# Two low-rank products of 256 columns for gate and up, their weight chunks paired, and a mixed order of the first sixteen chunks

## The chip, the cores and the metric

The kernel runs on one core of a Trainium2 chip. The metric is the device time of one execution in microseconds (us). Engines are TensorE (PE), VectorE (DVE), ScalarE (ACT), GpSimd (POOL) and SyncE (SP), each with its own instruction stream; SyncE issues most DMAs.

## The reference

Float32 throughout; 1024 tokens of width 512. Weights come as 4-bit NF4 codes (stored as int32) with one scale per 64 inputs, and each carries a low-rank product of rank 16.

```
W   = NF4[codes] * scale per block of 64
lin(x, W, A, B) = x W^T + (x A^T) B^T
q, k, v = lin(x, ...)            # 512 -> 512 each
x1 = x + lin((q + k + v) / 3, W_o, A_o, B_o)
h  = silu(lin(x1, W_gate, ...)) * lin(x1, W_up, ...)     # 512 -> 1792
y  = x1 + lin(h, W_down, ...)                            # 1792 -> 512
...   # then a second quantized layer (512 -> 512), a layer norm, a 4-batch attention
...   # with one head, a layer norm, and a top-16-of-64 mixture of rank-16 experts
```

The change touches only the first part, up to y. What follows it (the tail) is as before.

## The kernel before

The attention weights are folded into one matrix, M1 = (W_q + W_k + W_v)^T W_o^T / 3 + 1, with the low-rank products inside, so that x1 = M1 applied to x. A weight is decoded in **chunks** of 128x512. ScalarE and VectorE build the 16 NF4 levels out of clipped lines: for each chunk VectorE has four operations, `low` (L1469), `mid` (L1475), `clip` (L1482) and `out` (L1491, writes `value`), and ScalarE four that feed them (`bent` and `bank`, L895 and L917). GpSimd then multiplies by the scales (`wf`, L790 or L795; for k it also adds q, L800). There are 62 chunks: o0 to o3; q, k, v for each of four blocks of inputs; then gate, up and down (g, u, d) for fourteen slices f of 128 hidden units, and four chunks f of the second layer. A ring of three holds the codes (`code`, each 256 KB), loaded by SyncE; a slot is free when `mid` and the ScalarE step of `out` of the chunk before in it are done.

A precise product of 512 columns is three matmuls of float32r parts (hi*hi, hi*lo, lo*hi; `product`, L1114). After decoding, a chunk of gate, up or down gets its low-rank term: TensorE writes it to one PSUM bank (`lora`), VectorE adds it (`merge`, L1512 or L1515), ScalarE takes the hi part (`split`, L887) and GpSimd the lo part (L831). A low-rank product waits until the merge of the chunk before has freed the bank. For gate and up it is four matmuls of 128 columns (L1127), with A held as hi and lo rows in `la_gu` and B in `lb_gu`; `bprep` prepares these.

The order on VectorE, ScalarE and GpSimd is one list that all three walk (`vector_order`), on TensorE another (`tensor_order`). In the **front**, TensorE makes for each of the four blocks i: the low-rank sum of q, k, v (L1162), then two matmuls that add (q + k) and v (L1171, L1174) into a bank; `acc` splits it into `wq_hi` and `wq_lo`; twelve matmuls with the o weights and one with the identity give a block of M1; `m1` splits that (`m_hi`, `m_lo`); and nine matmuls (`partial`) apply it to the first 512 tokens. The other half of the tokens follows after the loop. Then come **rounds** f = 0 to 13: TensorE makes gate:2f, up:2f, gate:2f+1, up:2f+1 (12 matmuls each, for the two halves of the tokens), with low-rank products of the next chunks and down products of earlier slices (6 matmuls each) between them. Beside round f the other engines decode g, u and d of slice f+1. A gate or up chunk covers all 512 inputs of one of the two matrices.

## Time and profile before

| | us |
|---|---|
| time, median of 3 runs | 517.43 (516.74 to 517.47) |
| time of the profiled execution | 515.85 |
| its span in the profile | 514.0 |
| TensorE busy in the span | 482.7 |
| VectorE, ScalarE, GpSimd busy | 375.4, 291.0, 276.3 |

The span runs from the first to the last instruction; 1.85 us of the execution lie around it. The profiled execution is 1.58 us shorter than the median of the runs. An instruction's duration includes its pipeline: VectorE's of 128x512 are listed with some 0.68 us, and start 0.60 us apart when nothing is waited for.

### The profile page before, as it was taken

The numbers are of one execution on the slowest core, as the hardware profiler recorded it, in microseconds if no ns is written. First come the engines' busy times: TensorE is split into PE (matmuls) and PEld (weight loads), VectorE is DVE, ScalarE is ACT, GpSimd is POOL, SyncE is SP. The second block draws the span as 40 slices with busy tenths as digits, with TensorE's granted clock in tenths as the row PEclk, the third lists the DMA queues.
The fourth block names the chain that finished last, engine by engine and source line by source line (L and its number), as shares of the span: only waits on it lengthen the run. The fifth ranks groups of instructions, "written<-read, shape, count | busy, mean of one in ns | idle before, by whom it ended". The sixth has DMA issues, their size and how long they took to land.

```text
span 514.0 us, 7457 instructions
## 1 busy us (share of the span) xinstructions
PE 482.7 (94%) x2248; PEld 391.7 (76%) x2248; DVE 375.4 (73%) x707; ACT 291.0 (57%) x539; POOL 276.3 (54%) x255
## 2 busy tenths in 40 slices
PE   2488989999999999999999999999998999999995
PEld 1246668888888888888888888888886788888884
DVE  6979889847897887997979964884567946466433
ACT  6879868756655775765665733636586512333021
POOL 4786766776655775766665754756299210110001
PEclk9999999999999999999999999999999999999998
DMA  7664532613323332332433201730000000000011
GB/s 213 215 238 133 154 85 84 181 46 102 98 74 97 102 114 92 106 119 83 124 104 94 71 1 53 248 141 1 1 1 0 2 1 22 22 20 22 1 42 41
DMA packets 21415, 43.01 MB, mean 84 GB/s; under 512 B 3328, under 2 KB 3456, under 8 KB 21120
## 3 DMA queue, kind: packets, MB, share of 16 engines
q1 hardware_dynamic: 21152, 42.16, 26.6%
q0 software_dynamic: 224, 0.38, 0.3%
q8 instruction: 19, 0.31, 0.2%
q14 instruction: 20, 0.16, 0.1%
HBM read 40.42 MB, written 2.10 MB: 83 GB/s over the span
## 4 chain that ended last, share of the span: by engine, by line
PE 84%; DVE 4%; issue 4%; ACT 3%; POOL 1%; ACTq 0%; DVEq 0%; POOLq 0%
PE bank L1114 74%; PE bank L1282 2%; PE bank L1127 2%; PE bank L1402 1%; PE bank L1174 1%; ACT prob L1070 1%; PE bank L1136 1%; DVE rmax L1666 0%; ACT pT_hi L887 0%; PE bank L1162 0%; DVE bn L1620 0%; DVE pT_lo L1459 0%; PE bank L1315 0%; ACT eb_hi L887 0%; PE bank L1171 0%
## 5 line engine op out<-in xcount | busy, mean ns | idle before, releaser
L790 POOL TENSOR_TENSOR wf<-value,scale 128x512 f32<-128x512 f32 x50 | 64.6, 1291 | 70.4 <-DVE value L1491 70.1
L1114 PE MATMUL bank<-x_hi,gu_hi 128*128 128x512 f32 x224 | 88.5, 395 | 0.0
L1114 PE MATMUL bank<-x_lo,gu_hi 128*128 128x512 f32 x224 | 87.3, 390 | 0.0
L1114 PE MATMUL bank<-x_hi,gu_lo 128*128 128x512 f32 x224 | 87.3, 390 | 0.0
L870 POOL TENSOR_TENSOR rstd<-veps,neg_half 128x1 f32<-128x1 f32 x24 | 13.2, 550 | 110.8 <-issue 104.6
L895 ACT ACTIVATE bank<-code 128x512 f32<-128x512 int32 x124 | 68.7, 585 | 0.0
L1455 DVE TENSOR_TENSOR xs<-bank,xs 128x512 f32<-128x512 f32 x56 | 38.5, 687 | 23.9 <-PE bank L1114 23.4
L1469 DVE SCALAR_TENSOR_TENSOR low<-bent,bank 128x512 f32<-128x512 f32 x62 | 42.3, 682 | 12.0 <-ACT bank L895 7.4
L1114 PEld LDWEIGHTS bank<-x_hi,gu_lo 128*128 128x128 f32 x224 | 42.1, 188 | 8.8
L1114 PEld LDWEIGHTS bank<-x_lo,gu_hi 128*128 128x128 f32 x224 | 42.1, 188 | 7.9
L1114 PEld LDWEIGHTS bank<-x_hi,gu_hi 128*128 128x128 f32 x224 | 42.1, 188 | 7.9
L842 POOL TENSOR_TENSOR h_lo<-act_f,h_hi 128x512 fp32r<-128x512 f32 x28 | 36.3, 1297 | 20.9 <-ACT h_hi L887 20.9
L1482 DVE SCALAR_TENSOR_TENSOR low<-low,bank 128x512 f32<-128x512 f32 x62 | 42.5, 686 | 5.8
L887 ACT ACTIVATE h_hi<-act_f 128x512 fp32r<-128x512 f32 x28 | 17.7, 632 | 47.7 <-DVE act_f L1552 42.4
L1114 PE MATMUL bank<-h_hi,wd_hi 128*128 128x512 f32 x112 | 43.7, 390 | 0.0
L1114 PE MATMUL bank<-h_hi,wd_lo 128*128 128x512 f32 x112 | 43.6, 389 | 0.0
L1114 PE MATMUL bank<-h_lo,wd_hi 128*128 128x512 f32 x112 | 43.6, 389 | 0.0
L1475 DVE SCALAR_TENSOR_TENSOR bank<-code,bank 128x512 f32<-128x512 int32 x62 | 42.6, 687 | 1.1 <-ACT bank L917 0.7
L1491 DVE SCALAR_TENSOR_TENSOR value<-bank,low 128x512 f32<-128x512 f32 x62 | 42.3, 683 | 0.9 <-ACT bank L895 0.8
L895 ACT ACTIVATE bent<-code 128x512 f32<-128x512 int32 x62 | 38.4, 619 | 4.8 <-DMA code<-codes 4.8
L917 ACT ACTIVATE bank<-code 128x512 f32<-128x512 int32 x62 | 36.7, 592 | 3.2 <-DVE low L1482 3.2
L831 POOL TENSOR_TENSOR gu_lo<-wf,gu_hi 128x512 fp32r<-128x512 f32 x28 | 36.8, 1315 | 2.2 <-ACT gu_hi L887 1.9
(228 smaller groups left out, 1163.7 us busy)
## 6 DMA issues: line engine op xcount, KB each, us to landing
code<-codes SPq DMA_DIRECT2D x62, 256.0 KB, 2.7
scale<-scales SPq DMA_DIRECT2D x100, 128.0 KB, 3.0
xs<-xT SPq DMA_DIRECT2D x2, 1024.0 KB, 7.4
ea_raw<-ex_A SPq DMA_DIRECT2D x1, 2048.0 KB, 9.7
eb_raw<-ex_B SPq DMA_DIRECT2D x1, 2048.0 KB, 8.7
out<-rows SPq DMA_DIRECT2D x8, 256.0 KB, 2.0
bgu_raw<-loB_gu SPq DMA_DIRECT2D x1, 896.0 KB, 5.8
wqkv_raw<-w_qkv SPq DMA_DIRECT2D x1, 768.0 KB, 4.3
```

The costliest lines, as they stand in the source:

```text
L790: pool.tensor_tensor(w, v, scale[:, i % RING_CODES, :], ALU.mult).then_inc(scaled_done, 1)
L831: pool.tensor_tensor(lo, shaped(c, merged_at(c)), hi.bitcast(F32), ALU.subtract).then_inc(lo_done, 1)
L842: pool.tensor_tensor(h_lo[:, f % RING_H, hs], act_f[:, n % 2, :], h_hi[:, f % RING_H, hs].bitcast(F32), ALU.subtract).then_inc(hlo_done, 1)
L887: nc.scalar.activation(dst, src, ACT.Copy).then_inc(done, 1)
L895: nc.scalar.activation(dst, src, ACT.Prelu, bias=float(start), scale=float(slope), alpha=float(alpha)).then_inc(done, 1)
L917: nc.scalar.activation(mid_ps[:, :], code[:, j % RING_CODES, :], ACT.Relu, bias=float(RELU_MID[1]), scale=float(RELU_MID[0])).then_inc(mid ...
L1114: last = nc.tensor.matmul(ps, a, b, start=start and i == 0 and n == 0, stop=stop and i == len(terms) - 1 and n == 2)
L1455: nc.vector.tensor_tensor(xs[:, b, o, :], down_bank(gi, n)[:, :], xs[:, b, o, :], ALU.add)\
L1469: nc.vector.scalar_tensor_tensor(low[:, j % 2, :], bent[:, j % 2, :], float(BEND_LOW[3] - BEND_LAST[3]), last_ps[:, :], ALU.add, ALU.min). ...
L1475: nc.vector.scalar_tensor_tensor(mid_ps[:, :], code[:, j % RING_CODES, :], float(CODE_SHIFT), mid_ps[:, :], ALU.add, ALU.max).then_inc(mid ...
L1482: nc.vector.scalar_tensor_tensor(lj, lj, float(BEND_LAST[3]), mid_ps[:, :], ALU.add, ALU.min)\
L1491: nc.vector.scalar_tensor_tensor(value[:, j % 2, :], top_ps[:, :], float(BEND_TOP[3]), low[:, j % 2, :], ALU.add, ALU.max).then_inc(value_ ...
```

## The change

Five things.

1. **Pairing.** A gate or up chunk of slice f no longer holds one matrix for all inputs: chunk g holds both matrices for inputs 0 to 255, chunk u both for inputs 256 to 511. Each gate and up product waits for chunk g, makes six matmuls, waits for chunk u, and makes six more.
2. **Low-rank products.** With a chunk that holds both matrices, one stationary part of A serves 256 columns of B (gate and up side by side): two matmuls of 256 columns instead of four of 128. B is prepared in parts of three slices (`bprep` 1 to 5, of 128x768 or less) instead of two (128x512 and 128x1280), loaded as needed; A is half as wide.
3. **Order of the later chunks.** g2 moves ahead of round 1 and each g of slice f+2 stands beside round f, so the order beside round f is u, d of slice f+1 and g of slice f+2. Round 12 then has six half chunks beside it where it had eight. The order of round 1 changes too: `bprep` 2 goes ahead of g2, and merges and splits of g2 and u2 move up.
4. **Front order.** The first sixteen chunks are o0 o1 q0 o2 k0 o3 v0 and then q, k, v of blocks 1 to 3, with omerge, osplit, acc and m1 at other places; TensorE makes all nine matmuls of `partial` behind the two accumulating ones instead of three before them.
5. **Front loads.** The codes of the first sixteen chunks use four slots; the scales of o0 to o3 are issued one chunk at a time; x comes in eight pieces of 256 KB instead of two of 1 MB; A and B of o are loaded first and have a semaphore of their own; loads for gate, up and down come later and in smaller pieces.

```diff
+LAST_BEATS = [2, 0, 2, 0, 1, 0, 1, 0]
+def beside_round(f):
+    chunks = [("u", f + 1), ("d", f + 1), ("g", f + 2)]
+    return [c for c in chunks if c[1] < NF]
 def chunk_list():
-    chunks = [("o", k) for k in range(KT)] + [(m, i) for i in range(KT) for m in "qkv"]
-    chunks += [("g", 0), ("u", 0), ("g", 1), ("u", 1), ("d", 0), ("d", 1)]
+    chunks = [("o", 0), ("o", 1), ("q", 0), ("o", 2), ("k", 0), ("o", 3), ("v", 0)]
+    chunks += [(m, i) for i in range(1, KT) for m in "qkv"]
+    chunks += [("g", 0), ("u", 0), ("g", 1), ("u", 1), ("d", 0), ("d", 1), ("g", 2)]
     for f in range(1, NF):
-        chunks += [(m, f + 1) for m in "gud"] if f + 1 < NF else []
+        chunks += beside_round(f)
...
+FRONT = 4 * KT
+RING_FRONT = 4
...
-LB_FIRST = 4
-XSPLIT_AFTER = [6, 7, 8, 9, 11, 12, 13, 14]
+LB_PART = 3
+XSPLIT_AFTER = [7, 9, 10, 12, 13, 15]
+EXTRA_LOADS = {6: ["x0"], 8: ["x1"], 9: ["x2"], 11: ["x3"], 12: ["x4"], 13: ["x5", "gate_a"], 14: ["gate_b0"],
+               15: ["x6"], 16: ["x7"], 18: ["down"]}
+PART_LOADS = {("d", 0): 1, ("g", 3): 2, ("u", 6): 3, ("u", 9): 4}
...
     order.append(("low", CHUNKS[0]))
-    for j in range(4 * KT):
-        half(CHUNKS[j], 0)
+    merge_at = {2: 0, 3: 1, 5: 2, 7: 3}
+    for j in range(FRONT):
+        order.append(("mid", CHUNKS[j]))
+        if j in merge_at:
+            order.append(("omerge", merge_at[j]))
+        if j in (10, 13):
+            order.append(("m1", (j - 10) // 3))
+        order += [("clip", CHUNKS[j]), ("low", CHUNKS[j + 1])]
+        if j in merge_at:
+            order.append(("osplit", merge_at[j]))
+        if j in (8, 11, 14):
+            order.append(("acc", (j - 8) // 3))
+        order.append(("out", CHUNKS[j]))
         if j == 3:
             order.append(("eyes", 0))
-        half(CHUNKS[j], 1)
         if j in XSPLIT_AFTER:
             order.append(("xsplit", XSPLIT_AFTER.index(j)))
-    due.clear()
     def alone(c, *parts):
         for part in parts or (0, 1):
             half(c, part)
         due.clear()
-    alone(("g", 0))
-    order.append(("acc", KT - 1))
-    alone(("u", 0), 0)
-    order.append(("bprep", 0))
-    alone(("u", 0), 1)
-    order += [("bprep", 1), ("m1", KT - 1)]
-    alone(("g", 1), 0)
-    order += [("x1", 0), ("x1", 1)]
+    order += [("mid", ("g", 0)), ("m1", KT - 2), ("clip", ("g", 0)), ("low", ("u", 0)), ("out", ("g", 0)), ("xsplit", 6),
+              ("mid", ("u", 0)), ("acc", KT - 1), ("clip", ("u", 0)), ("low", ("g", 1)), ("out", ("u", 0)), ("bprep", 0),
+              ("mid", ("g", 1)), ("clip", ("g", 1)), ("m1", KT - 1), ("bprep", 1), ("xsplit", 7), ("x1", 0), ("x1", 1)]
...
-    order.append(("silu", 0))
+    order += [("silu", 0), ("bprep", 2)]
...
-    alone(("d", 2), 0)
-    order += [("hsplit", 1), ("low", ("g", 3)), ("split", ("d", 1)), ("out", ("d", 2)), ("silu", 2)]
-    due += [[2, ("merge", ("d", 2))], [3, ("split", ("d", 2))]]
-    order += [("merge", ("g", 2)), ("split", ("g", 2)), ("h", 2), ("merge", ("u", 2)), ("hsplit", 2), ("silu", 3),
-              ("split", ("u", 2)), ("bprep", 2)]
+    order += [("mid", ("d", 2)), ("merge", ("g", 2)), ("clip", ("d", 2)), ("hsplit", 1), ("low", ("g", 3)),
+              ("split", ("d", 1)), ("out", ("d", 2)), ("split", ("g", 2)), ("silu", 2), ("mid", ("g", 3)),
+              ("merge", ("u", 2)), ("clip", ("g", 3)), ("h", 2), ("split", ("u", 2)), ("hsplit", 2), ("silu", 3)]
+    due += [[1, ("merge", ("d", 2))], [2, ("split", ("d", 2))]]
+    half(("g", 3), 1)
...
+        if f in (3, 6, 9):
+            order.append(("bprep", 2 + f // 3))
...
-        for step, count in zip(steps, BEATS[len(halves)]):
+        for step, count in zip(steps, LAST_BEATS if f == NF - 2 else BEATS[len(halves)]):
...
-            beside = [*ahead[:2], None, None]
+            beside = [("g", 2), ahead[0], ahead[1], None]
         elif late:
-            beside = [ahead[0], ahead[1], ahead[2], None]
+            beside = [*ahead, None] if len(ahead) == 3 else [ahead[0], None, ahead[1], None]
...
+        code_fourth = at("code_fourth", 128, [P, 512], I32)
...
+            for j in range(RING_FRONT):
+                load_code(j)
+                if j >= 2:
+                    load_scale(CHUNKS[j - 2])
+            for j, c in enumerate(CHUNKS):
+                if j < RING_FRONT:
+                    continue
+                for name in EXTRA_LOADS.get(j, []):
+                    load_extra(name)
+                if c in PART_LOADS:
+                    load_extra(f"gate_b{PART_LOADS[c]}")
...
+                sp.wait_ge(mid_done, code_before(j) + 1)
+                sp.wait_ge(top_ready, code_before(j) + 1)
+                load_code(j)
+                if j == 5:
+                    load_scale(("o", 2))
+                elif j == 6:
+                    load_scale(("o", 3))
+                elif j >= FRONT:
+                    load_scale(c)
...
+            pool.dma_start(la_o[:, :], loA_o).then_inc(olora_in, 16)
+            pool.dma_start(lb_o[:, :], loB_o).then_inc(olora_in, 16)
             pool.dma_start(sc_qkv[:, :, :], scales_qkv).then_inc(sqkv_in, 16)
             pool.dma_start(ident[:, :], eye).then_inc(eye_in, 16)
-            pool.dma_start(la_o[:, :], loA_o).then_inc(lora_in, 16)
-            pool.dma_start(lb_o[:, :], loB_o).then_inc(lora_in, 16)
...
-                    pe.wait_ge(bprep_done, 2 if k < LB_FIRST else 3)
-                    for h in range(KT):
-                        last = nc.tensor.matmul(lora_ps[:, h * P:(h + 1) * P],
-                                                la_gu[:, "gu".index(kind), h * P:(h + 1) * P],
-                                                lb_gu[:, k * P:(k + 1) * P], start=True, stop=True)
+                    pe.wait_ge(bprep_done, 2 + k // LB_PART)
+                    for h in range(2):
+                        m = 2 * "gu".index(kind) + h
+                        last = nc.tensor.matmul(lora_ps[:, 2 * h * P:2 * (h + 1) * P], la_gu[:, m * P:(m + 1) * P],
+                                                lb_gu[:, k // LB_PART % 2, k % LB_PART, :, :], start=True, stop=True)
...
-                if i:
-                    pe.wait_ge(m1hi_done, i)
-                    pe.wait_ge(m1lo_done, i)
-                    pe.wait_ge(xhi_done, i)
-                    pe.wait_ge(xlo_done, i)
-                    partial(i - 1, 0)
...
                 if i:
-                    partial(i - 1, 1)
-                    partial(i - 1, 2)
+                    pe.wait_ge(m1hi_done, i)
+                    pe.wait_ge(m1lo_done, i)
+                    pe.wait_ge(xhi_done, i)
+                    pe.wait_ge(xlo_done, i)
+                    for r in range(KT - 1):
+                        partial(i - 1, r)
...
-                pe.wait_ge(hi_done, split_no(("gu"[g], f)))
-                pe.wait_ge(lo_done, split_no(("gu"[g], f)))
                 s, ps = f % RING_GU, unit_ps[m % 3][:, :]
-                product(ps, [(gu_hi[:, s, g, k, :], gu_lo[:, s, g, k, :], x1_hi[:, k, tk], x1_lo[:, k, tk])
-                             for k in range(KT)]).then_inc((gate_ready, unit_ready)[g], 1)
+                for h in range(2):
+                    pe.wait_ge(hi_done, split_no(("gu"[h], f)))
+                    pe.wait_ge(lo_done, split_no(("gu"[h], f)))
+                    last = product(ps, [(gu_hi[:, s, k, g, :], gu_lo[:, s, k, g, :], x1_hi[:, k, tk], x1_lo[:, k, tk])
+                                        for k in (2 * h, 2 * h + 1)], start=h == 0, stop=h == 1)
+                last.then_inc((gate_ready, unit_ready)[g], 1)
...
+            half = slice(2 * "gu".index(kind), 2 * "gu".index(kind) + 2)
+            codes.append(cg[:, cut].reshape(2, P, KT, P).transpose(3, 2, 0, 1)[:, half].reshape(P, H))
```

On SyncE at the start of the program the issues stand so before:

```order
L707 DMA code<-codes 128x512 x3
L736 DMA scale<-scales 64x512 x6
L728 DMA code<-codes 128x512
L736 DMA scale<-scales 64x512 x2
L728 DMA code<-codes 128x512 x3
L711 DMA xs<-xT 128x4x512
L728 DMA code<-codes 128x512 x2
```

and so after the change:

```order
L748 DMA code<-codes 128x512 x3
L757 DMA scale<-scales 64x512 x2
L748 DMA code_fourth<-codes 128x512
L757 DMA scale<-scales 64x512 x2
L748 DMA code<-codes 128x512 x2
L757 DMA scale<-scales 64x512 x2
L765 DMA xs<-xT 128x512
L748 DMA code<-codes 128x512
L757 DMA scale<-scales 64x512 x2
L748 DMA code_fourth<-codes 128x512
```

The fourth codes go out behind one pair of scales instead of three, and pieces of x stand between the codes.

On VectorE, in the last block of the front, from `mid` of chunk v3 on, before (L1530 is m1:2, L1459 is acc:3):

```order
L1475 SCALAR_TENSOR_TENSOR bank<-code,bank 128x512
L1482 SCALAR_TENSOR_TENSOR low<-low,bank 128x512
L1469 SCALAR_TENSOR_TENSOR low<-bent,bank 128x512
L1491 SCALAR_TENSOR_TENSOR value<-bank,low 128x512
L1530 SCALAR_TENSOR_TENSOR m_lo<-bank,m_hi 128x512
L1475 SCALAR_TENSOR_TENSOR bank<-code,bank 128x512
L1482 SCALAR_TENSOR_TENSOR low<-low,bank 128x512
L1469 SCALAR_TENSOR_TENSOR low<-bent,bank 128x512
L1491 SCALAR_TENSOR_TENSOR value<-bank,low 128x512
L1459 TENSOR_TENSOR wq_lo<-bank,wq_hi 128x512
```

and after the change, from the same `mid`:

```order
L1544 SCALAR_TENSOR_TENSOR bank<-code_fourth,bank 128x512
L1551 SCALAR_TENSOR_TENSOR low<-low,bank 128x512
L1538 SCALAR_TENSOR_TENSOR low<-bent,bank 128x512
L1560 SCALAR_TENSOR_TENSOR value<-bank,low 128x512
L1544 SCALAR_TENSOR_TENSOR bank<-code,bank 128x512
L1599 SCALAR_TENSOR_TENSOR m_lo<-bank,m_hi 128x512
L1551 SCALAR_TENSOR_TENSOR low<-low,bank 128x512
L1538 SCALAR_TENSOR_TENSOR low<-bent,bank 128x512
L1560 SCALAR_TENSOR_TENSOR value<-bank,low 128x512
L1544 SCALAR_TENSOR_TENSOR bank<-code,bank 128x512
L1528 TENSOR_TENSOR wq_lo<-bank,wq_hi 128x512
```

Both splits have moved one operation later, so that they wait less for TensorE.

On ScalarE, the stretch from the SiLU of gate:8 (the first act_f) to that of gate:9, beside round 4, before:

```order
L994 ACTIVATE act_f<-bank 128x512
L895 ACTIVATE bent<-code 128x512
L895 ACTIVATE bank<-code 128x512 x2
L917 ACTIVATE bank<-code 128x512
L887 ACTIVATE h_hi<-act_f 128x512
L887 ACTIVATE wd_hi<-wf 128x512
L895 ACTIVATE bent<-code 128x512
L895 ACTIVATE bank<-code 128x512 x2
L917 ACTIVATE bank<-code 128x512
L887 ACTIVATE gu_hi<-wf 128x512
L994 ACTIVATE act_f<-bank 128x512
```

and after the change:

```order
L1062 ACTIVATE act_f<-bank 128x512
L960 ACTIVATE bent<-code 128x512
L960 ACTIVATE bank<-code 128x512 x2
L982 ACTIVATE bank<-code 128x512
L952 ACTIVATE h_hi<-act_f 128x512
L952 ACTIVATE gu_hi<-wf 128x512
L960 ACTIVATE bent<-code 128x512
L960 ACTIVATE bank<-code 128x512 x2
L982 ACTIVATE bank<-code 128x512
L952 ACTIVATE gu_hi<-wf 128x512
L1062 ACTIVATE act_f<-bank 128x512
```

Before, this stretch splits d4 and then g5; after the change it splits g5 and then u5, so the split of u5 stands where that of g5 stood.

## Rows read from the trace of the kernel before

**Rows 1.** Busy time by stretch; each engine's us and (xinstructions).

```profile
core 0: us, PE busy (x) PEld busy (x) DVE busy (x) ACT busy (x) POOL busy (x), PEclk, DMA share, GB/s
0.00:66.50 66.50, 43.65 (x139) 27.00 (x139) 53.84 (x90) 54.32 (x103) 46.17 (x47) 1.00 0.61 189
66.50:367.00 300.50, 300.02 (x1405) 249.98 (x1406) 238.57 (x386) 182.58 (x333) 192.16 (x157) 1.00 0.31 94
367.00:514.00 147.00, 138.99 (x706) 114.72 (x704) 83.02 (x233) 54.10 (x104) 37.98 (x52) 0.99 0.04 15
```

**Rows 2.** Waits of TensorE: engine line waited for: us, times, longest.

```profile
PE bank L1155 <- DMA lb_qkv<-loB_qkv: 9.4, 1, 9.4
PE bank L1171 <- POOL wf L800: 7.6, 1, 7.6
...
PE bank L1114 <- DVE wq_lo L1459: 1.7, 2, 1.5
```

**Rows 3.** VectorE in time: start us, us, instruction, idle before and releaser.

```profile
4.48 0.69 DVE L1469 SCALAR_TENSOR_TENSOR low<-bent,bank 128x512 f32<-128x512 f32 x1 [3.29 <-ACT bank L895]
...
11.59 0.69 DVE L1498 SCALAR_TENSOR_TENSOR wf<-wf,bank 128x512 f32<-128x512 f32 x1 [0.63 <-PE bank L1155]
...
26.37 0.69 DVE L1469 SCALAR_TENSOR_TENSOR low<-bent,bank 128x512 f32<-128x512 f32 x1 [1.29 <-ACT bank L895]
26.97 0.68 DVE L1491 SCALAR_TENSOR_TENSOR value<-bank,low 128x512 f32<-128x512 f32 x1
...
31.57 0.69 DVE L1459 TENSOR_TENSOR wq_lo<-bank,wq_hi 128x512 fp32r<-128x512 f32 x1 [0.41 <-ACT wq_hi L887]
...
38.38 0.69 DVE L1530 SCALAR_TENSOR_TENSOR m_lo<-bank,m_hi 128x512 fp32r<-128x512 f32 x1 [1.55 <-ACT m_hi L958]
...
51.76 0.69 DVE L1459 TENSOR_TENSOR wq_lo<-bank,wq_hi 128x512 fp32r<-128x512 f32 x1 [0.17 <-ACT wq_hi L887]
...
61.04 0.69 DVE L1459 TENSOR_TENSOR wq_lo<-bank,wq_hi 128x512 fp32r<-128x512 f32 x1 [0.83 <-ACT wq_hi L887]
```

**Rows 4.** ScalarE in time, the two waits for a code chunk.

```profile
11.51 0.63 ACT L895 ACTIVATE bent<-code 128x512 f32<-128x512 int32 x1 [1.72 <-DMA code<-codes]
...
25.16 0.63 ACT L895 ACTIVATE bent<-code 128x512 f32<-128x512 int32 x1 [2.04 <-DMA code<-codes]
```

**Rows 5.** SyncE's DMA queue in time: issues.

```profile
2.10 3.73 SPq L736 DMA_DIRECT2D scale<-scales  x6
6.52 0.34 SPq L728 DMA_DIRECT2D code<-codes  x1
...
16.99 0.60 SPq L711 DMA_DIRECT2D xs<-xT  x1
```

**Rows 6.** TensorE in time, one matmul of the first pass and the last two passes.

```profile
28.83 2.08 PE L1174 MATMUL bank<-wf,unit_eye 128*128 128x512 f32 x2 [0.56 <-POOL wf L795]
...
52.60 0.47 PE L1114 MATMUL bank<-wo_hi,wq_hi 128*128 128x512 f32 x1
...
55.75 1.16 PE L1162 MATMUL bank<-la_qkv,lb_qkv 48*128 48x128 f32 x8
57.72 0.47 PE L1114 MATMUL bank<-x_hi,m_hi 128*128 128x512 f32 x1 [0.81 <-issue]
...
61.87 0.47 PE L1114 MATMUL bank<-wo_hi,wq_hi 128*128 128x512 f32 x1
...
66.53 0.47 PE L1114 MATMUL bank<-x_hi,m_hi 128*128 128x512 f32 x1 [1.46 <-ACT m_hi L958]
```

**Rows 7.** TensorE in time, around one low-rank product of up.

```profile
81.42 0.39 PE L1114 MATMUL bank<-x_hi,m_lo 128*128 128x512 f32 x1
81.65 0.56 PE L1127 MATMUL bank<-lb_gu,la_gu 128*128 128x128 f32 x4
82.05 0.45 PE L1114 MATMUL bank<-x_hi,m_hi 128*128 128x512 f32 x1
82.33 0.40 PE L1114 MATMUL bank<-x_lo,m_hi 128*128 128x512 f32 x1
```

**Rows 8.** Every low-rank product of gate and up.

```profile
L1127 PE MATMUL bank<-lb_gu,la_gu x112: 218/274/327, 68.7 to 292.0; 128*128 128x128 f32 x112
```

**Rows 9.** TensorE, then VectorE and GpSimd in time, round 1 and gate:4.

```profile
98.89 0.56 PE L1127 MATMUL bank<-lb_gu,la_gu 128*128 128x128 f32 x4
...
108.08 0.39 PE L1114 MATMUL bank<-x_hi,gu_hi 128*128 128x512 f32 x1
...
97.90 0.68 DVE L1512 SCALAR_TENSOR_TENSOR wf<-wf,bank 128x512 f32<-128x512 f32 x1
...
102.97 1.29 POOL L831 TENSOR_TENSOR gu_lo<-wf,gu_hi 128x512 fp32r<-128x512 f32 x1
...
106.76 1.30 POOL L831 TENSOR_TENSOR gu_lo<-wf,gu_hi 128x512 fp32r<-128x512 f32 x1 [1.26 <-ACT gu_hi L887]
```

**Rows 10.** GpSimd and below it TensorE in time, chunks and products of round 5.

```profile
154.89 1.30 POOL L831 TENSOR_TENSOR gu_lo<-wf,gu_hi 128x512 fp32r<-128x512 f32 x1
...
160.87 1.31 POOL L831 TENSOR_TENSOR gu_lo<-wf,gu_hi 128x512 fp32r<-128x512 f32 x1
...
159.12 0.39 PE L1114 MATMUL bank<-x_hi,gu_hi 128*128 128x512 f32 x1
...
163.43 0.39 PE L1114 MATMUL bank<-x_hi,gu_hi 128*128 128x512 f32 x1
```

150 lines of the change are left out of this document (82 added, 68 removed).

## The prediction

> **What bounds the kernel now.** I read first the busy time by stretch [rows 1]. It has three parts. From 66.5 to 367 us TensorE is busy 300.02 of 300.5 us: time goes there only if TensorE has less to do. Before 66.5 it is busy 43.65 us, with VectorE at 53.84 and ScalarE at 54.32: here the engines wait for each other. The tail from 367 on is not touched and moves as a whole. Next the waits of TensorE [rows 2]: 9.4 us until the B of q, k and v has landed, 7.6 us until GpSimd has added q0 and k0, then only short ones. The early waits are those of an engine with little to do yet. So I went to VectorE in order of time [rows 3], because a chunk takes four of its operations and it starts one each 0.60 us (26.37 to 26.97). With 0.2 us more where `clip` directly follows `mid`, a chunk is 2.6 us, and sixteen chunks with the splits between them fill most of the front. The rows show where it stood: 0.63 us for the first low-rank product of o, 1.29 us in chunk k1, 0.41, 1.55, 0.17 and 0.83 us for the loop with TensorE. ScalarE's rows name the cause of some: it waited 1.72 and 2.04 us for codes [rows 4], which stood in SyncE's queue behind six scale loads (3.73 us of issuing) and behind 1 MB of x [rows 5]. Last, TensorE's last two passes of the attention loop [rows 6], which set when the saturated part begins.
>
> **The front.** (a) Until the first `wq_lo`. In the new order it is 40 operations behind the first `low`, which starts at 4.48 [rows 3]: the codes of o0 still come first. Five of the chunks before it have `clip` directly behind `mid`. 4.48 + 40 x 0.60 + 5 x 0.2 = 29.5 us, if no chunk waits for codes; the four small ScalarE copies of the identity may cost a few tenths, so 29.5 to 30.1, where it started at 31.57. That is 1.5 to 2.1 us. The codes: four slots give each load one chunk (2.6 us) more, and x stands between them in quarters, so I take both code waits of [rows 4] as gone. TensorE, still slow there, needs what it needed from `wq_lo` 0 to `m_lo` 0 (31.57 to 38.38, 6.8 us), so `m_lo` 0 comes at about 36.6. It stands one operation later than before, and so costs less waiting.
> (b) From there to the `wq_lo` of block 2 the new order has 21 operations on VectorE: 12.6 us and 0.6 for three direct `clip`s, 13.2 us, ending at 49.8 where it was 51.76. Gain 1.9 us.
> (c) Then TensorE sets the pace. From the first of twelve matmuls of block 2 to that of block 3 it took 61.87 - 52.60 = 9.27 us, in which it stood 0.81 us before `partial`, waiting for `m_lo` [rows 6]. Now `partial` comes behind the two accumulating products, when `m_lo` is there: 8.46 us. VectorE's `wq_lo` of block 3 is 12 operations behind that of block 2, 7.6 us, so it is not late. Gain 1.9 + 0.8 = **2.7 us** when the saturated part begins. Its bounds: 1.5 (only the first step's low end holds) and 3.8 (a late `m_lo` costs nothing either).
> What could be new: q1 overwrites k0 in the ring of three `wf` and so waits for the accumulation of block 0; TensorE ends that about 2.1 us after v0 is scaled (its slow pair of matmuls [rows 6]), just when VectorE delivers q1. I price it at nothing; half a microsecond would be hidden in the wait for `m_lo` 0.
>
> **The low-rank products.** One now costs 0.45 us: from 81.42 to 82.33 TensorE starts what would take two steps of 0.23 us without it, 0.91 - 0.46 [rows 7]. There are 28 (112 matmuls in groups of four) [rows 8]. The four start 0.10 us apart, where a matmul of four times the columns takes 0.23: columns are not what paces them. A float32r matmul of 256 columns isn't in the trace. The nearest rows bound it: 0.10 us (as with 128) and 0.23 (as with 512). Half of the 512 one is 0.114; I take 0.12. Two cost 0.24 us, so each product saves 0.21; bounds 0 and 0.25.
> Where does it count? Not in the first four. After the front VectorE's list runs without a gap into round 1: the merge of d1 starts at 97.90 and ends at 98.58, and TensorE begins the product of g2, which must wait for it, at 98.89 [rows 9]. VectorE doesn't get shorter there, so what g0, u0 and g1, u1 save turns into a wait at d1's or g2's product. `bprep` 2, now ahead of g2, puts about 0.9 us on ScalarE and 1.9 on GpSimd into this stretch (768 columns, one and a half times the 0.63 of [rows 4] and the 1.30 of [rows 10]); the first delays VectorE by perhaps 0.4 us, and this eats a part of the next savings. I count 24 products: 24 x 0.21 = **5.0 us**, bounds 0 and 6.
>
> **Rule against row.** The Trainium skill (TensorE: Matmul & The Clock Gate, Back-to-back issue gap) gives 134 cycles for a matmul of 128 columns and 262 for one of 256. By it four of the first and two of the second differ by 12 cycles, 5 ns, and the change would save 0.1 us in all; the row's 0.10 us a matmul is nearly twice the page's figure, so I hold the number of matmuls, not of columns, for the price.
>
> **Pairing.** Gate:10 starts at 159.12 and up:10 at 163.43 [rows 10]. Before, u5 was complete at 160.87 + 1.31 = 162.18, 1.25 us ahead of up:10. Paired, u5 is wanted in the middle of gate:10, 159.12 + 6 x 0.23 = 160.5. But its split now stands where that of g5 stood, which was complete at 154.89 + 1.30 = 156.2. Slack 4.3 us: cost nothing, hidden under up:9 and a down product. The same holds in the other rounds, as the order is the same rotated by one chunk. Two waits more per product are on semaphores long passed. The three later `bprep` steps (again 0.9 us of ScalarE and 1.9 of GpSimd) fall where these are busy 183 and 192 of 300 us [rows 1]: nothing. The new place of round 12's chunks changes no TensorE work: nothing. In round 2 the codes of g3 wait in SyncE's queue for `bprep` 2 and 384 KB more; up to 1 us late. The lo parts of g2 and u2 came at 104.3 and 108.06 and gate:4 started at 108.08 [rows 9]; u2 now stands directly behind g2 on GpSimd, 1.3 us later, so with that delay too near 107, 2.4 us before the middle of gate:4.
>
> **Sum.** 2.7 + 5.0 = 7.7 us. The profiled execution took 515.85 us, so 508.2; it was 1.6 us under the median of the runs, and against 517.43 the forecast is 509.7.
>
> **Rivals.**
> - *Columns pace the low-rank products.* Two matmuls of 256 columns then cost what four of 128 do, and only the front is left: 517.4 - 2.7 = 514.7. For it: the true rate at 256 columns of float32r isn't shown, and 0.10 us for 128 columns is also twice the rate of the 512 row, as if a narrow matmul ran at half rate. Against: weight loads, one per matmul, explain the 0.10 as well.
> - *The front gains nothing.* The loop of acc, split, twelve matmuls and m1 goes through four engines, and later places on VectorE may only move its waits; or smaller x loads still delay codes. Then 5.0 us: 512.4. Against: both code waits and the 0.81 us are plain.
> - *Slower: gate waits for its second half.* If u comes when it came before, each gate product stands 162.18 - 160.5 = 1.7 us; over 12 rounds 20 us, less 7.7: 530. It decides from 0.64 us a round on (7.7 / 12). For it: VectorE, ScalarE and GpSimd now must be a chunk ahead, and round 1 is tight. Against: the 4.3 us of slack; they must first be lost to codes that come late.
> - *Better on both.* The upper bounds hold: front 3.8 us, products 6: 507.6. For it: the front is bounded by VectorE only where I assumed it is. Against: each upper bound needs the others' waits to vanish too.
>
> **Chances.** Forecast 0.62, columns 0.11, front without gain 0.11, better on both 0.08, slower 0.07, and 0.01 for less than either. The likeliest case alone spans 507.5 to 512. For 8 in 10 the range is 506.8 to 514.3. I call within 0.2% (516.4 to 518.5) no change, about what a measurement can tell: faster 0.89, same 0.04, slower 0.07.
>
> **What would show it.** The low-rank products of gate and up in time: two steps of 0.12 us. VectorE in the front: no wait for codes in chunks o2 to q2, first `wq_lo` near 30, that of block 2 near 50, TensorE's first twelve of block 3 near 59, saturation from 64 on. TensorE's waits: a few tenths before d1's or g2's product, none before a gate's seventh matmul. It is wrong if TensorE is idle more than 1 us between 70 and 360, or if the low-rank product still takes 0.4 us.

## The result and the profile after

The changed kernel takes 512.59 us (median of 4 runs, 512.24 to 513.5) against 517.09 (516.5 to 517.47) of the kernel before on the same chip: ratio 0.9919, 95% interval 0.9903 to 0.9934, 4.5 us by the medians. The two profiled executions have spans of 514.0 and 510.5, 3.5 us apart. The forecast was 509.7, a gain of 7.7; so a good half of it came. The traces account for the 3.5; the kernel before varies more from run to run than the changed one, and where the 1.0 us between the spans and the medians lies isn't shown. I look for what is missing in the order of the forecast.

Busy time by stretch, as in [rows 1], cut where TensorE starts the last first-layer pass and where the tail begins:

```profile
core 0: us, PE busy (x) PEld busy (x) DVE busy (x) ACT busy (x) POOL busy (x), PEclk, DMA share, GB/s
0.00:64.70 64.70, 42.64 (x139) 26.68 (x139) 54.68 (x91) 53.71 (x103) 43.71 (x45) 1.00 0.63 178
64.70:363.00 298.30, 296.66 (x1347) 243.00 (x1348) 236.84 (x384) 184.26 (x337) 197.75 (x161) 1.00 0.34 100
363.00:510.50 147.50, 139.51 (x708) 115.25 (x706) 83.59 (x233) 54.63 (x105) 37.99 (x52) 1.00 0.04 15
```

In the long stretch TensorE was busy in all but 0.48 us before and is now idle for 1.64. In the kernel before it alone was the limit; now something else is too. Its waits (engine, line waited for, us, times, longest) name the two places:

```profile
PE bank L1223 <- DMA lb_o<-loB_o: 6.2, 1, 6.2
PE bank L1182 <- DVE wq_lo L1528: 5.0, 3, 3.0
PE bank L1234 <- POOL wf L865: 3.8, 1, 3.8
PE bank L1231 <- ACT gain_eye L992: 3.4, 1, 3.4
PE bank L1237 <- POOL wf L860: 2.2, 1, 2.2
...
PE bank L1196 <- DVE wf L1584: 0.9, 2, 0.6
...
PE bank L1204 <- DVE wf L1581: 0.4, 1, 0.4
...
PE bank L1204 <- DVE wf L1584: 0.2, 1, 0.2
```

Most long ones of the front lie ahead of its first product, where TensorE has little to do, as before. New are three waits for `wq_lo` of 5.0 us (3.0 for block 0, 1.01 each for blocks 1 and 2) where the two of [rows 2] came to 1.7 us, and waits of low-rank products (L1196, L1204) for VectorE's merge.

**Front.** VectorE in time, the rows that answer to [rows 3]:

```profile
31.20 0.68 DVE L1528 TENSOR_TENSOR wq_lo<-bank,wq_hi 128x512 fp32r<-128x512 f32 x1
...
37.39 0.69 DVE L1599 SCALAR_TENSOR_TENSOR m_lo<-bank,m_hi 128x512 fp32r<-128x512 f32 x1 [1.72 <-ACT m_hi L1023]
...
41.96 0.68 DVE L1528 TENSOR_TENSOR wq_lo<-bank,wq_hi 128x512 fp32r<-128x512 f32 x1
...
51.26 0.68 DVE L1528 TENSOR_TENSOR wq_lo<-bank,wq_hi 128x512 fp32r<-128x512 f32 x1
...
59.13 0.69 DVE L1528 TENSOR_TENSOR wq_lo<-bank,wq_hi 128x512 fp32r<-128x512 f32 x1
```

and TensorE, the first of the twelve matmuls of blocks 1, 2 and 3 and the first of the last `partial`:

```profile
42.79 0.47 PE L1182 MATMUL bank<-wo_hi,wq_hi 128*128 128x512 f32 x1 [1.01 <-DVE wq_lo L1528]
...
52.09 0.47 PE L1182 MATMUL bank<-wo_hi,wq_hi 128*128 128x512 f32 x1 [1.01 <-DVE wq_lo L1528]
...
60.18 0.39 PE L1182 MATMUL bank<-wo_hi,wq_hi 128*128 128x512 f32 x1
...
64.74 0.47 PE L1182 MATMUL bank<-x_hi,m_hi 128*128 128x512 f32 x1 [1.46 <-ACT m_hi L1023]
```

The first `wq_lo` comes at 31.20 (forecast 29.5 to 30.1, before 31.57), that of block 2 at 51.26 (forecast 49.8, before 51.76), the twelve of block 3 at 60.18 (before 61.87), and the last `partial` at 64.74 (before 66.53): 1.8 us, where 2.7 was forecast.

**Low-rank products.** TensorE around three of them, one of the first passes, that of g8, and one of a down chunk; then all those of gate and up, with the idle time ahead of their matmuls and weight loads (before the change 1.6 us in three places and 0.3 in two):

```profile
76.27 0.39 PE L1182 MATMUL bank<-x_hi,m_lo 128*128 128x512 f32 x1
76.50 0.40 PE L1196 MATMUL bank<-lb_gu,la_gu 128*128 128x256 f32 x2
76.73 0.40 PE L1182 MATMUL bank<-x_hi,m_hi 128*128 128x512 f32 x1
...
187.15 0.39 PE L1182 MATMUL bank<-h_hi,wd_lo 128*128 128x512 f32 x1
187.64 0.51 PE L1196 MATMUL bank<-lb_gu,la_gu 128*128 128x256 f32 x2
187.98 0.40 PE L1182 MATMUL bank<-x_hi,gu_hi 128*128 128x512 f32 x1
...
205.05 0.50 PE L1204 MATMUL bank<-lb_dp,la_dp 128*128 128x512 f32 x1
205.39 0.40 PE L1182 MATMUL bank<-x_hi,gu_hi 128*128 128x512 f32 x1
```

```profile
L1196 PE MATMUL bank<-lb_gu,la_gu x56: 277/282/388, 66.9 to 284.5; 128*128 128x256 f32 x56
...
  DVE wf L1584: 3.9, 7
  DVE wf L1581: 1.3, 4
```

The first takes 76.73 - 76.50 = 0.23 us, as forecast: two matmuls of 256 columns cost what one of 512 does. The other two take 187.98 - 187.64 = 0.34 and 205.39 - 205.05 = 0.34, and the g8 one starts 0.26 us late on top (187.64 less 187.15 + 0.23).

**Where the time went, round by round.** (after is the changed kernel; the others are the experiments.) The first matmul of gate:0, gate:2 and so on marks the start of a round; the differences of these times, us:

```
round           gate:0 at    0     1     2     3     4     5     6     7     8     9    10    11    12
before             84.83 11.34 11.91 16.11 17.47 17.46 17.70 17.49 17.93 17.50 17.95 17.47 17.92 17.53
after              82.46 12.00 11.82 16.72 17.07 17.25 17.30 17.47 17.67 17.46 17.66 17.47 17.64 17.13
e128               83.49 11.39 12.25 16.11 17.47 17.46 17.86 17.69 17.88 17.70 17.88 17.69 17.87 17.10
accearly           80.44 12.06 11.82 16.30 17.07 17.25 17.30 17.48 17.66 17.44 17.66 17.45 17.64 17.11
bprep_late         82.54 11.63 11.79 16.60 17.07 17.26 17.30 17.46 17.66 17.45 17.64 17.45 17.66 17.11
loralate           82.98 12.06 11.80 16.60 17.07 17.28 17.30 17.11 17.66 17.36 17.69 17.35 17.66 17.11
all3               80.55 11.60 11.81 16.94 17.06 17.26 17.30 17.13 17.64 17.38 17.64 17.36 17.64 17.10
spin_even          83.66 12.02 11.81 16.52 17.07 17.26 17.30 17.65 17.64 17.67 17.64 17.65 17.64 17.12
spin_odd           82.39 12.04 11.82 16.23 17.06 17.26 17.30 17.46 17.84 17.48 17.85 17.45 17.64 17.13
oldloads           84.94 11.33 11.80 16.40 17.07 17.29 17.30 17.47 17.64 17.46 17.64 17.46 17.64 17.12
relief             83.47 12.03 11.81 16.62 17.07 17.29 17.30 17.10 17.49 17.11 17.49 17.11 17.49 16.85
usplit             82.86 12.03 11.82 16.21 17.07 17.26 17.29 17.14 17.67 17.14 17.65 17.15 17.65 16.85
prodlate           79.44 11.64 11.80 16.59 17.07 17.06 17.07 17.33 17.26 17.32 17.26 17.33 17.26 17.07
all5               79.70 11.63 11.81 16.56 17.07 17.07 17.06 17.33 17.26 17.33 17.26 17.32 17.26 17.07
```

Rounds 1 to 12 should each have lost 0.42 us (two products by 0.21). Rounds 3, 5 and 12 do (0.40), round 12 only because it now has one gate or up product less. Round 4 loses 0.21, rounds 7, 9 and 11 some 0.28, rounds 6, 8 and 10 nothing, round 1 only 0.09, as it now also has the product of d2 (0.23), and rounds 0 and 2 became longer by 0.66 and 0.61. Against 0.42 a round the largest losses are thus those of rounds 0 and 2, 1.7 us together; rounds 6, 8 and 10 lose 1.2, rounds 7, 9 and 11 0.4, rounds 1 and 4 0.5. Rounds 0 to 12 together are 1.12 us shorter; 2.37 us were won by gate:0, 1.8 in the front and 0.6 by three of the four products of the first passes (the second waits).

### The profile page after: what moved, and what is told of

Its sections match the earlier page's. It is cut to its first block, busy times and chain, and to the rows that moved or that the text cites. A ratio compares the mean times of both kernels' runs of the same rounds, so it can differ in the third digit from the quotient of the medians.

```text
span 510.5 us, 7422 instructions
## 1 busy us (share of the span) xinstructions
PE 478.8 (94%) x2192; PEld 384.9 (75%) x2192; DVE 375.1 (73%) x707; ACT 292.6 (57%) x542; POOL 279.4 (55%) x258
## 4 chain that ended last, share of the span: by engine, by line
PE 67%; DVE 4%; issue 3%; ACT 2%; POOL 0%; ACTq 0%; DVEq 0%
PE bank L1182 60%; PE bank L1351 3%; PE bank L1471 1%; PE bank L1196 1%; PE bank L1204 1%; ACT prob L1138 1%; DVE rmax L1735 0%; ACT pT_hi L952 0%; DVE bn L1689 0%; DVE pT_lo L1528 0%; PE bank L1384 0%; DVE value L1560 0%; ACT eb_hi L952 0%; PE bank L1383 0%; DVE xb_lo L1528 0%
## 5 line engine op out<-in xcount | busy, mean ns | idle before, releaser
L935 POOL TENSOR_TENSOR rstd<-veps,neg_half 128x1 f32<-128x1 f32 x24 | 13.2, 551 | 110.8 <-issue 104.6
L960 ACT ACTIVATE bank<-code 128x512 f32<-128x512 int32 x116 | 64.7, 586 | 0.0
L1544 DVE SCALAR_TENSOR_TENSOR bank<-code,bank 128x512 f32<-128x512 int32 x58 | 39.8, 687 | 2.4 <-ACT bank L982 2.1
L960 ACT ACTIVATE bent<-code 128x512 f32<-128x512 int32 x58 | 35.9, 619 | 2.2 <-DMA code<-codes 2.2
L982 ACT ACTIVATE bank<-code 128x512 f32<-128x512 int32 x58 | 34.3, 591 | 1.9 <-DVE low L1551 1.7
```

Source lines behind the costliest of these rows:

```text
L960: nc.scalar.activation(dst, src, ACT.Prelu, bias=float(start), scale=float(slope), alpha=float(alpha)).then_inc(done, 1)
L982: nc.scalar.activation(mid_ps[:, :], code_at(j), ACT.Relu, bias=float(RELU_MID[1]), scale=float(RELU_MID[0])).then_inc(mid_ready, 1)
L1544: nc.vector.scalar_tensor_tensor(mid_ps[:, :], code_at(j), float(CODE_SHIFT), mid_ps[:, :], ALU.add, ALU.max).then_inc(mid_done, 1)
```

## The experiments

Theory: the low-rank product is as cheap as forecast, but VectorE now runs so close to TensorE that a part of each saving turns into a wait for a merge; and in the front the later `acc` gives back what the new order wins. Rival: the sum of the forecast was right in kind and some independent trouble (codes, `bprep`) takes 3 us. Ratios are to runs of the kernel before on the same chip at the same time. That kernel varies from 514.0 to 518.3 us from run to run, by 3 to 4 us on one chip, and its median from 515.4 to 517.1 from one set of runs to the next. By the intervals two ratios less than about 0.003 apart can't be told from each other. What a change does is therefore read mostly from the table.

**e128: the narrow product back.**

```diff
-last = nc.tensor.matmul(lora_ps[:, 2 * h * P:2 * (h + 1) * P], la_gu[...], lb_gu[..., k % LB_PART, :, :], ...)
+for g in range(2):
+    last = nc.tensor.matmul(lora_ps[:, (2 * h + g) * P:(2 * h + g + 1) * P], la_gu[...], lb_gu[..., k % LB_PART, g, :], ...)
```

> The changed kernel with one thing undone: each of the two low-rank matmuls of 256 columns is two of 128 again, so a low-rank product of gate or up should cost TensorE about 0.45 us instead of 0.24. Theory (the saving of a product is real but a part of it is given back in waits for VectorE, because in rounds 6, 8 and 10 VectorE's thirteen operations between two merges end as late as before): only about 1 to 2.5 us slower than the changed kernel, 513.7 to 515. Rival (the sum of my forecast: each of 24 products counts in full): 5.0 us slower or more, 517.6.

515.19 us, ratio 0.9982 (0.997 to 0.9994); span 513.3, so the wide product is worth 2.8 us by the spans and 3.3 by the ratios (0.0063 of 517), between both expectations. Of the 2.8, 0.4 is chance of this execution's front (its last `partial` starts at 65.16, that of the changed kernel at 64.74; see the last section). The table says where: rounds 3 (17.47 against 17.07) and 5 get two or more products back, rounds 4 and 6 to 11 only one (0.21 to 0.24), round 12 none; round 1 gets two (0.43), and rounds 0 and 2 are 0.61 shorter than in the changed kernel. It also isolates the rest of the change: e128 against before costs 0.34 us in round 1 (a down product more) and 0.2 in rounds 6, 8 and 10, nothing in 2, 3 and 4, and wins 0.43 in round 12, which has one product less (round 5 has it now, at 0.16).

**accearly: acc before clip.**

```diff
+        if j in (8, 11, 14):                      # behind ("mid", CHUNKS[j])
+            order.append(("acc", (j - 8) // 3))
-        if j in (8, 11, 14):                      # behind ("low", ...)
-            order.append(("acc", (j - 8) // 3))
```

> The changed kernel with the acc operation of VectorE two operations earlier in blocks 0 to 2 (directly behind mid), as the front had it before. Theory (the late acc makes TensorE stand 1.01 us for wq_lo ahead of the twelve matmuls of blocks 1 and 2, which is what ate step (b) of the forecast): 0.8 to 2 us faster, 510.6 to 511.8, the twelve matmuls of block 3 start at 59.2 or earlier instead of 60.18. Rival (VectorE then waits for TensorE's product at acc instead, so that the chain through TensorE sets the pace either way): within 0.3 us, 512.3 to 512.9, with a wait of VectorE for TensorE in front of acc.

509.97 us, ratio 0.9875 (0.9853 to 0.9898), span 508.1: 2.4 us under the changed kernel, more than the theory had. In the table 2.0 of it lie ahead of gate:0 and 0.4 in round 2. VectorE:

```profile
29.86 0.68 DVE L1528 TENSOR_TENSOR wq_lo<-bank,wq_hi 128x512 fp32r<-128x512 f32 x1
...
36.94 0.69 DVE L1599 SCALAR_TENSOR_TENSOR m_lo<-bank,m_hi 128x512 fp32r<-128x512 f32 x1 [1.41 <-ACT m_hi L1023]
...
40.11 0.68 DVE L1528 TENSOR_TENSOR wq_lo<-bank,wq_hi 128x512 fp32r<-128x512 f32 x1
...
48.68 0.69 DVE L1528 TENSOR_TENSOR wq_lo<-bank,wq_hi 128x512 fp32r<-128x512 f32 x1
...
57.25 0.69 DVE L1528 TENSOR_TENSOR wq_lo<-bank,wq_hi 128x512 fp32r<-128x512 f32 x1
```

From 36.94 to 60.44 VectorE lists no wait and starts an operation every 0.60 us, or after 0.79 where `clip` directly follows `mid`; `wq_lo` follows `wq_lo` by 8.57 us, which is its fourteen operations, where the changed kernel had 9.30 (41.96 to 51.26). TensorE doesn't wait for `wq_lo` of blocks 1 to 3 at all. The two operations between `mid` and `acc` lay on the loop acc, twelve matmuls, m_hi, m_lo. Not all of the 0.73 us a block is that loop: `m_lo` no longer comes 0.34 late for `m_hi`, but `acc` now also stands between `mid` and `clip`, which saves the 0.2 of a direct `clip` on VectorE alone.

**bprep_late: bprep 2 out of round 0.**

```diff
-PART_LOADS = {("d", 0): 1, ("g", 3): 2, ("u", 6): 3, ("u", 9): 4}
+PART_LOADS = {("d", 0): 1, ("u", 4): 2, ("u", 6): 3, ("u", 9): 4}
-    order += [("silu", 0), ("bprep", 2)]
+    order.append(("silu", 0))
-    ... ("hsplit", 2), ("silu", 3)]
+    ... ("hsplit", 2), ("bprep", 2), ("silu", 3)]
```

> The changed kernel with bprep 2 moved from round 0 to behind the split of h of round 2, and the load of the third part of gate's B with it, from the codes of g3 to those of u4. Theory (bprep 2 delays the merge of d1 in round 0, and its raw load holds up the codes of g3 for round 2): both stretches lose their waits, 1.0 to 1.3 us faster, 511.3 to 511.6; ScalarE's 0.85 us wait for the codes of g3 is gone and TensorE's 0.4 us wait in front of d1's product too. Rival (the engines catch up or wait at the next product anyway): 0 to 0.4 us faster.

512.67 us, ratio 0.9927 (0.9908 to 0.9946), span 510.0: 0.5 us less by the spans and nothing by the medians, so the rival (0 to 0.4) is nearer. Round 0 falls by 0.37, as expected; round 2 hardly (0.12). The wait for codes (ScalarE of the changed kernel, 98.12) is gone, but VectorE, first of the changed kernel, then of this one,

```profile
98.12 0.63 ACT L960 ACTIVATE bent<-code 128x512 f32<-128x512 int32 x1 [0.85 <-DMA code<-codes]
...
106.58 0.69 DVE L1538 SCALAR_TENSOR_TENSOR low<-bent,bank 128x512 f32<-128x512 f32 x1 [2.25 <-ACT bent L960]
```

```profile
106.16 0.69 DVE L1539 SCALAR_TENSOR_TENSOR low<-bent,bank 128x512 f32<-128x512 f32 x1 [3.08 <-ACT bent L961]
```

waits 0.83 us more for ScalarE further on, since `bprep` 2 now stands there. That late codes of g3 lengthen round 2 is seen across kernels in which it is alike (but for e128's narrow products): they waited 0.20 (e128), 0.33 (usplit), 0.36 (spin_odd), 0.42 (accearly), 0.52 (oldloads), 0.61 (spin_even), 0.68 (loralate), 0.75 (relief) and 0.85 us (after) for them, and round 2 took 16.11, 16.21, 16.23, 16.30, 16.40, 16.52, 16.60, 16.62 and 16.72. It grows nearly one for one. But with the wait at 0.33 the round is still no shorter than before (16.11): what else holds it there isn't shown. In each of them VectorE waits those 2.25 us for ScalarE.

**loralate: the product ahead of the second up goes behind it in rounds 6, 8, 10 and 12.**

```diff
-            if beside[2 * b] and (late and b == 0 or b):
+            if beside[2 * b] and (late and b == 0 or b) and not (late and b):
                 order.append(("lora", beside[2 * b]))
             order.append(("up", 2 * f + b))
+            if beside[2 * b] and late and b:
+                order.append(("lora", beside[2 * b]))
```

> The changed kernel with the low-rank product that stands beside the second half of a gate chunk (of g8 and its like) moved behind the up chunk in rounds 6, 8, 10 and 12. Theory (in these rounds the saving is given back only because this product waits for VectorE's merge where it stands): 0.6 to 1.4 us faster, 511.2 to 512.0. Rival (VectorE itself is the bound of these rounds, so the wait only moves to the next product or down chunk): within 0.3 us of the changed kernel, 512.3 to 512.9.

512.39 us, ratio 0.9923 (0.9905 to 0.9941), span 510.5, as the changed kernel: by the times the rival holds. By the table round 6 is shorter by 0.36, but 8 and 10 by 0.11 only, as the other gate product of these rounds then costs 0.5; these 0.6 us don't show in the span, because this execution's front was 0.5 longer. The wait vanishes where another doesn't take its place.

**spin_even and spin_odd: one more operation on VectorE.**

```diff
+            if f in SPIN_ROUNDS and step == ("h", 2 * f):     # (6, 8, 10) or (5, 7, 9)
+                order.append(("spin", f))
+                elif kind == "spin":
+                    nc.vector.bn_stats(spun[:, item[1], :], x1_hi[:, 0, :512].bitcast(F32))
```

> The changed kernel with one more operation of 512 columns on VectorE (about 0.6 us) behind the h of rounds 6, 8 and 10, which is inside the thirteen operations ahead of the merge that the low-rank product of g8 and its like waits for. Theory (VectorE sets the length of these rounds): each of them gets 0.5 to 0.6 us longer, 1.5 to 1.8 in all. Rival (TensorE sets it and the waits of 0.2 us are chance): 0 to 0.3 us in all.

> The changed kernel with the same extra operation behind the h of rounds 5, 7 and 9. Theory (VectorE has slack in the six half chunks of these rounds): 0 to 0.4 us in all; round 5, in which no product waited, doesn't change. Rival (VectorE is the bound everywhere in the long stretch): 1.5 to 1.8 us as for the even rounds.

Ratios 0.9941 (0.9923 to 0.996) and 0.993 (0.9905 to 0.9954). Rounds 6, 8 and 10 grow by 0.18 to 0.21 each, not by 0.6; rounds 7 and 9 by 0.17 and 0.19, round 5 not at all. So my theory for the even rounds was a third right: VectorE limits them, but not alone. Of the 0.6 us some 0.3 fill a wait of VectorE for ScalarE inside the thirteen operations (185.70, below), and a tenth was slack. The odd rounds came out within 0 to 0.4 in all, as expected, but rounds 7 and 9 grow as much each as the even ones: the pair of runs doesn't show that VectorE has more room in them.

**oldloads: the front's loads as before.**

This is near the old loads, not the same: x stays in pieces, four issued in a row, and four scale loads instead of six stand ahead of the fourth codes.

```diff
-RING_FRONT = 4
+RING_FRONT = 3
-EXTRA_LOADS = {6: ["x0"], 8: ["x1"], 9: ["x2"], 11: ["x3"], 12: ["x4"], 13: ["x5", "gate_a"], ...
+EXTRA_LOADS = {7: ["x0", "x1", "x2", "x3"], 13: ["x4", "x5", "x6", "x7", "gate_a"], ...
...
-                    load_scale(CHUNKS[j - 2])
+                    load_scale(("o", 0))
+                    load_scale(("o", 1))
```

> The changed kernel with the loads of the front as they were before: three slots for the codes, x in its two large bunches, the scales of o behind the first codes. The new order of VectorE and of TensorE stays. Theory (the waits for codes are real and went away by the new loads, and VectorE's chain from the first low to the first wq_lo is what counts): ScalarE waits for codes again in the front, 1.0 to 2.5 us in all, and the first wq_lo comes at 32.0 to 33.0 instead of 31.20; the whole 0.5 to 1.5 us slower. Rival (the code waits were idle time that cost nothing, since the loop with TensorE in blocks 1 and 2 sets the pace): within 0.3 us of the changed kernel, 512.3 to 512.9.

513.98 us, ratio 0.9953 (0.9933 to 0.9973), span 512.0. ScalarE waits 0.57 and 1.52 us for codes (before 1.72 and 2.04), VectorE behind it 1.13 at 25.73, and the first `wq_lo` comes at 32.43, 1.23 later; gate:0 2.48 later, of which rounds 0 and 2 give 1.0 back. The loads are worth 1.5 us or so, and without them the new order of chunks wins nothing in the front (gate:0 at 84.94, before 84.83).

**relief: VectorE's down additions narrowed in rounds 6 to 11.** The kernel leaves out 448 of the 512 columns of each.

```diff
+w = 64 if 15 <= gi * NB * KT + n <= 38 else 512
-nc.vector.tensor_tensor(xs[:, b, o, :], down_bank(gi, n)[:, :], xs[:, b, o, :], ALU.add)
+nc.vector.tensor_tensor(xs[:, b, o, :w], down_bank(gi, n)[:, :w], xs[:, b, o, :w], ALU.add)
```

> The changed kernel, in which VectorE's additions of the down product in rounds 6 to 11 take 64 columns instead of 512, so that it has about 0.5 us less to do in each of four places a round; it leaves out the rest of these additions. By the products' costs in the changed kernel, TensorE loses 0.16 to 0.40 us a round from round 6 on at low-rank products. Theory (these losses come from VectorE alone): rounds 6, 8 and 10 fall from 17.47 to about 17.1 and rounds 7, 9 and 11 from 17.65 to 17.5; together 1.2 to 1.6 us. Rival (the merges are late because of ScalarE and GpSimd ahead of VectorE): at most 0.4 us in all.

511.11 us, ratio 0.9912 (0.9884 to 0.994). Rounds 6 to 12 are 17.10, 17.49, 17.11, 17.49, 17.11, 17.49 and 16.85: together 1.86 us less, and each product costs 0.23 to 0.26. This is the forecast's saving in full, so what was missing from round 6 on is VectorE's load. The median is 1.5 us under the changed kernel's, but the ratio only 0.0007 lower; the span is 0.9 lower, because this execution's front was 1.0 us longer (gate:0 at 83.47; the last section says why).

**usplit: the split of each up chunk half a chunk later.**

```diff
-                due.append([3, ("split", c)])
+                due.append([4 if c[0] == "u" and c[1] > 3 else 3, ("split", c)])
```

> The changed kernel with the split of each up chunk from u4 on half a chunk later (about 2.2 us) on ScalarE, and with it on GpSimd. My forecast put the slack of the second half of a pair at 4.3 us and the cost of pairing at nothing. If that is right, nothing changes beyond 0.2 us in all, and no seventh matmul of a gate waits. Rival (the second half comes just in time): up to 2 us in each of the rounds 3 to 11, 5 to 18 us in all.

511.31 us, ratio 0.9921 (0.9892 to 0.9949), span 509.2. The slack was there, and the move uses nearly all of it. In the changed kernel u4 was complete at 137.30 and u5 at 154.91, 4.1 and 3.8 us ahead of the seventh matmul of their gate. Here the split came 4.0 and 3.3 us later, not 2.2, and GpSimd (first row) ends u4 at 141.30:

```profile
139.99 1.31 POOL L896 TENSOR_TENSOR gu_lo<-wf,gu_hi 128x512 fp32r<-128x512 f32 x1
...
141.12 0.39 PE L1182 MATMUL bank<-x_hi,gu_lo 128*128 128x512 f32 x1
141.45 0.47 PE L1182 MATMUL bank<-x_hi,gu_hi 128*128 128x512 f32 x1
```

The second matmul is the seventh of gate:8. It starts 0.33 us behind the sixth instead of 0.23, so it is 0.10 late; for u5 to u12 0.3 to 3.9 us are left. Not expected: rounds 6, 8, 10 and 12 fall to 17.14 and 16.85, as far as in relief. VectorE from the down addition to the merge of d7, changed kernel and usplit:

```profile
178.94 0.69 DVE L1524 TENSOR_TENSOR xs<-bank,xs 128x512 f32<-128x512 f32 x1 [0.46 <-PE bank L1182]
...
184.72 0.69 DVE L1551 SCALAR_TENSOR_TENSOR low<-low,bank 128x512 f32<-128x512 f32 x1
185.70 0.69 DVE L1538 SCALAR_TENSOR_TENSOR low<-bent,bank 128x512 f32<-128x512 f32 x1 [0.29 <-ACT bank L960]
...
186.91 0.68 DVE L1581 SCALAR_TENSOR_TENSOR wf<-wf,bank 128x512 f32<-128x512 f32 x1
```

```profile
178.86 0.69 DVE L1524 TENSOR_TENSOR xs<-bank,xs 128x512 f32<-128x512 f32 x1 [0.47 <-PE bank L1182]
...
184.64 0.69 DVE L1551 SCALAR_TENSOR_TENSOR low<-low,bank 128x512 f32<-128x512 f32 x1
185.25 0.68 DVE L1538 SCALAR_TENSOR_TENSOR low<-bent,bank 128x512 f32<-128x512 f32 x1
...
186.45 0.68 DVE L1581 SCALAR_TENSOR_TENSOR wf<-wf,bank 128x512 f32<-128x512 f32 x1
```

In the changed kernel `low` at 185.70 waits 0.29 us for ScalarE's `bank`, because the split of u7 stood ahead of the code operations there. With the split behind them VectorE runs through, the merge ends 0.4 us earlier, and g8's product doesn't wait. So it is VectorE's thirteen operations plus this one wait that cost the even rounds their saving. Rounds 7, 9 and 11 stay at 17.65: their down product still costs 0.34.

**all3, prodlate and all5: put together.** all3 joins accearly, bprep_late and loralate. prodlate adds, from round 4 on, that a low-rank product goes behind the gate or up product that it stood ahead of; all5 moves `m1` of block 0 as well:

```diff
+    while at > start:                             # prodlate, over the finished order, from ("gate", 8)
+        if order[at][0] == "lora" and order[at + 1][0] in ("gate", "up"):
+            order[at], order[at + 1] = order[at + 1], order[at]
+        at -= 1
-        if j in (10, 13):                         # all5
-            order.append(("m1", (j - 10) // 3))
+        if j == 13:
+            order.append(("m1", 1))
...
         order.append(("out", CHUNKS[j]))
+        if j == 10:
+            order.append(("m1", 0))
```

> The changed kernel with three of the edits tried before together: acc two operations earlier in blocks 0 to 2, bprep 2 behind the split of h of round 2 (and the load of its part with the codes of u4), and the low-rank product beside a late half chunk behind up. Theory (the three act in places of their own and add up: 2.4, 0.5 and 0 to 0.6 us by the spans of the three kernels): span 507.0 to 507.6, time 508.9 to 509.5, 1.4 to 1.6% under the kernel before. Rival (what one saves the next gives back at the following wait of TensorE for VectorE, since VectorE is the bound of rounds 6 to 10): the time of the early acc alone, 509.9 to 510.3.

> The combined kernel with, from round 4 on, each low-rank product that stands directly ahead of a gate or up product put behind it. Theory (a product costs 0.36 to 0.53 us instead of 0.24 where VectorE's merge of the chunk before ends just when TensorE arrives, and 2.7 us later the merge is long done): all products cost 0.24, 0.8 to 1.4 us less over rounds 4 to 12, span 506.4 to 507.0, time about 508.2. Rival (VectorE's own merge then waits for the later product and passes the wait on): within 0.3 us of the combined kernel, 509.2.

> The kernel with the later products and, in the front, m1 of block 0 three operations of VectorE later (behind the out of the same chunk), where VectorE waited 1.60 us for ScalarE's m_hi. Theory (VectorE is without a gap from there to 60 us, so what it doesn't wait there is gained, up to where the accumulated product of block 1 is not ready before about 39.4): 0.6 to 1.2 us less than the kernel with the later products alone. Rival (acc of block 1 takes the wait over whole): within 0.2 us of it.

all3: 509.17 us, ratio 0.986 (0.9835 to 0.9885), span 507.8, 0.3 under accearly. The time lies in the theory's range and the span just above it, but the parts don't add up: round 0 and rounds 6, 8, 10 keep what they won, and round 2 grows to 16.94 (accearly 16.30), so all rounds together are only 0.36 shorter than accearly's. prodlate: 507.33 us, ratio 0.9839 (0.9814 to 0.9865), span 504.9. All products cost 0.24 from round 3 on; rounds 3 to 12 take 172.0 us where all3 had 173.5, slightly more than the 1.4 expected at most; another 1.1 us lie ahead of gate:0, where the two kernels are alike (8 slow matmuls instead of 12, last section). all5: 506.65 us, ratio 0.9832 (0.9806 to 0.9857), span 505.1. In the front the wait for `m_hi` is gone, and `acc` of block 1 waits instead:

```profile
37.01 0.68 DVE L1614 SCALAR_TENSOR_TENSOR m_lo<-bank,m_hi 128x512 fp32r<-128x512 f32 x1
...
39.39 0.69 DVE L1543 TENSOR_TENSOR wq_lo<-bank,wq_hi 128x512 fp32r<-128x512 f32 x1 [1.10 <-ACT wq_hi L967]
```

The intervals of prodlate and all5 overlap almost wholly, and the fronts of the two profiled executions differ by chance too (8 and 11 slow matmuls), so the last move can't be told from nothing. Both beat the kernel before by 1.6 to 1.7%; the changed kernel does by 0.8%.

## Why the prediction was right in kind and too large

- **Front, (a):** the first `wq_lo` was 1.1 to 1.7 us later than counted. The code waits did go (oldloads brings both back in part). The count missed that VectorE started 0.31 us later (4.79) and waited for ScalarE 0.62 us at 17.43, behind the copies of the identity that were priced at a few tenths, and 0.35 at 29.20. TensorE then took 6.2 us to `m_lo` 0 instead of 6.8, because its step to the faster pace came early (last section): luck, which hid 0.6 of the error.
- **Front, (b), the step that failed:** I counted VectorE's 21 operations from `m_lo` 0, 13.2 us, and took VectorE as the limit. The `wq_lo` of block 2 came at 51.26 instead of 49.8, a gain of 0.5 instead of 1.9. Of the 1.46 us missing 0.8 were there at `m_lo` 0 (37.39 instead of 36.6), from (a); 0.67 came in the 21 operations (13.87 us), half of it before `m_lo` 1, which waited for `m_hi`. With `acc` behind `clip` and `low`, TensorE waited 1.01 us for `wq_lo` in blocks 1 and 2: a loop through four engines with two operations too many in it. The change itself had moved `acc` there, and the forecast's sum put no price on it. This was the rival "the front gains nothing" in half measure; accearly shows it, 2.0 us ahead of gate:0, and with it VectorE is the limit that I had assumed.
- **Front, (c):** 8.09 us instead of 8.46 from block 2 to block 3, a gain of 1.2 instead of 0.8.
- **Low-rank product:** 0.24 forecast, 0.23 to 0.24 measured. The columns rival is out: half of the 512 row was right. By the cycle counts of the Trainium skill (TensorE: Matmul & The Clock Gate, Back-to-back issue gap), which are for a matmul by itself, the number of matmuls would hardly have counted. The same section says that at few columns they are too low for matmuls that each load weights, and that agrees better: e128, which changes only that number, has 0.45 us a product in place of 0.24 and is 2.8 us slower, so the measurement decides against the counts for these float32r matmuls.
- **"I count 24 products": the term that was mis-sized.** Of 5.0 us, 1.7 arrived (1.12 in the rounds and 0.6 before them, where I had counted none). The forecast charged only the first four products with VectorE, which was busy 239 of 300 us [rows 1]. On average it has room; but from round 6 on, between a down addition and the merge that the next low-rank product waits for, it has thirteen operations, 8.65 us with a wait of 0.29, against 8.4 us of TensorE. The forecast used this very argument for the first four products and not for the rest. relief and prodlate each remove this loss in another way, and usplit that of the even rounds. That is 1.6 us; another 1.7 lie in rounds 0 and 2 (below), 0.5 in rounds 1 and 4. The forecast's own sign of a wrong one, TensorE idle more than 1 us between 70 and 360, came: it was idle 1.60 of these 290 us.
- **Pairing at nothing:** the slack of 4.3 us held from round 3 on (3.8 to 6.7 us; 2.4 for gate:4, as forecast). usplit spends nearly all of it and costs one matmul 0.10. That "the order is the same rotated by one chunk" was wrong: which chunk's merge falls beside the h operations changed, and e128 shows 0.2 us in each of rounds 6, 8 and 10.
- **`bprep` 2 and the codes of g3:** round 0's wait came about where it was foreseen, and took back the savings ahead of it (12.00 against 11.39 in e128). The codes came 0.85 us late, within the "up to 1 us"; that this was hidden was wrong. It explains 0.5 us of round 2; why the round saves nothing even with a short wait stays open. I looked whether u2 would be in time for gate:4 (it was) and not at h:2 and the merge of g3, which went late behind them.
- **Rival "gate waits for its second half":** seen in no run but usplit, where it is 0.10 us.

## What to carry to other kernels

When work is taken from the engine that is the limit, look for the stretches in which the next engine's chain between two handshakes is already as long: an average of 79% busy says nothing about thirteen operations in a row. A handshake whose producer ends just in time can be moved one piece of work later if its consumer has slack; look in the trace by how much it really moved, as usplit's 4.0 us instead of 2.2 show. Here moving `acc`, two places on one list, gave 2.0 to 2.4 us, about as much as the wide product. In a loop through several engines, count the operations that stand between a result and its next consumer on each engine's list before counting the operations of one engine.

## What the runs showed of the hardware

TensorE's first matmuls after the idle time start 0.43 us apart and later ones 0.23. 512 columns in 0.43 us are 1.2 a nanosecond, in 0.23 us 2.2, so I read these as the clock's two levels, 1.2 and 2.4 GHz. In the changed kernel the step is at 35.4 us, in spin_even, the same up to there, not before 37.3:

```profile
34.73 0.63 PE L1182 MATMUL bank<-wo_hi,wq_hi 128*128 128x512 f32 x1
35.16 0.44 PE L1182 MATMUL bank<-wo_lo,wq_hi 128*128 128x512 f32 x1
35.43 0.40 PE L1182 MATMUL bank<-wo_hi,wq_lo 128*128 128x512 f32 x1
```

```profile
36.47 0.63 PE L1186 MATMUL bank<-wo_lo,wq_hi 128*128 128x512 f32 x1
36.90 0.63 PE L1186 MATMUL bank<-wo_hi,wq_lo 128*128 128x512 f32 x1
37.33 0.41 PE L1258 MATMUL bank<-three_eye,ident 128*128 128x128 f32 x1
```

The profile's granted clock is 1.00 through all of it. In the kernels with the same front the first twelve matmuls hold 7 slow ones (after), 8 (bprep_late, spin_odd), 10 (e128, loralate), 11 (usplit) or 12 (spin_even, relief), and `m_lo` of block 0 follows, from 37.33 us with 8 to 38.62 with 12 (0.4 of this was there at the first `wq_lo`). That is up to 1.3 us of chance in one execution's front, as much as the effects here. The kernel before had 10 in its profiled execution, the changed one 7: against loralate with 10 (gate:0 at 82.98) the front was worth 84.83 - 82.98 - 0.6 = 1.3 us, not 1.8; accearly had 11, so against usplit with 11 its front was worth 2.4. What makes the step come early or late stays open.

A product that TensorE starts right as VectorE's merge ends (at 204.99) costs 0.34 us instead of 0.23 even where no wait is listed (205.05, above). In prodlate, where these stand later, the 0.11 is gone. Whether it is the price of the handshake or a short wait that the profile doesn't list, no run here separates.
